# A four-layer transformer kernel on one core: re-ordered joined finish, outputs and first items loaded one stage early, and no start value in the counters of four stages

## The chip, the core and the metric

The kernel is one program on one core of a Trainium2 chip. Its time is the device time of one execution in microseconds (us), smaller is better. The engines are named as in the profile: PE (matmuls), DVE (vector), ACT (activations), POOL (GpSimd) and SP, the engine that in this kernel issues every DMA. They work side by side and wait for each other through semaphores.

## What is computed

Four residual blocks on x of shape 4 x 1024 x 128, cut from the reference:

```
x = x + LN(attn0(LN(x)))      # 16 heads of 8, scores clipped to +-10, causal softmax, output projection
x = x + LN(ffn0(LN(x)))       # RMS norm, latent attention with RoPE, RMS norm, 8 experts top 2 and a shared one
x = x + LN(attn1(LN(x)))      # 16 heads of 8, causal softmax
x = x + LN(ffn1(LN(x)))       # low rank: 128 -> 32 -> 512, gelu, 512 -> 32 -> 128
```

## The kernel before

**Stages.** After a setup (weights loaded, two of them folded together) the program runs nine stages, each a block of five instruction streams, with a barrier over all engines between two stages (`end_phase`, which also gives the semaphores back):

- p0 `project_heads8`: LN of x, q, k and v of attn0, each q and k split into three bf16 parts, stored to device memory (`q8_d`, `k8_d`, `v8_d`)
- a0 `attention`, clipped: 16 items of 4 heads of one sequence; outputs go to `o_d`
- fp `finish_and_project_latent`: joins the end of attn0 (softmax division, output projection, LN, residual add) with the start of ffn0 (RMS norm, latent projections, RoPE products and sums)
- am latent attention, fl its finish, me the experts
- p1 `project_heads8`, a1 `attention` (unclipped: it also finds the row maxima first), ff `finish_and_ffn`

The stages p0, p1, fp and ff go over 8 chunks of 512 tokens; the attentions go over 16 items. `x_res` holds x in SBUF throughout.

**What sets the order.** Nothing schedules: each engine runs its instructions in the order in which the code writes them. In p0 and p1 SP stores every chunk with 7 DMAs (one of v, three of q, three of k). An item of a0 or a1 is loaded with 25 DMAs (`load`, L695 and L698), two items ahead of its use. Before the change the first stretch of an attention's SP stream loads items 0 and 1; in a1 it then also writes eight small rows of minus ones (L737) from a tile that POOL sets (L955).

**The joined finish.** fp and ff are software pipelines. In step c of fp (c from -4 to 7) different chunks are in different phases: outputs of chunk c+4 are turned by PE (L1175) and divided by DVE (`normalise`, L1368 and L1372), chunk c+3 is turned (L391), copied by ACT (`copy_normalised`, L1257) and projected (L1192) into one PSUM bank, chunk c+2 gets its LN: statistics by DVE (L261, L270), `norm1.inverse` by POOL (L284 to L293), `apply_act` by ACT (L309), residual add by POOL (`add`, L1303). Chunk c+1 gets statistics of the new x (L1422, L1429), `inverse_rms` by POOL (L1315 to L1322), `apply_rms` by ACT (L1264) and is turned by PE. Chunk c is projected (four slots, L1226), multiplied with the RoPE tables by DVE (L1378), summed by POOL (`join`, L1330) and stored by SP. The output loads (L1126 in fp, L1875 in ff: 512 KB each) are issued inside the stage.

**Counters.** `sem` takes a semaphore and lets SP add BASE = 1 to it, so that every wait is for a value above 1; a stage's first work on the other engines waits for the last of these adds (`s_begin`). L86 is that add.

Of the kernel before, what the change touches and what calls it, by code (L numbers as in the profile page):

```python
# [17 lines left out]
P = 128  # L18
# [57 lines left out]
def build(nc, ins, consts, out):  # L76
    stack = ExitStack()
    with stack:
# [3 lines left out]
        phase_sems = []  # L82

        def sem(name):
# [66 lines left out]
        area_at = [0]  # L151

        def work(*shape, dt=F32, parts=P):

            n = int(np.prod(shape))
            words = n if dt == F32 else (n + 1) // 2
            a = area[0:parts, area_at[0]:area_at[0] + words]
# [18 lines left out]
        with nc.Block() as block:  # L176
# [8 lines left out]
            def _(pool):  # L185
                nc.gpsimd.memset(zero_f[:, :], 0.0).then_inc(c_zero, 1)
                nc.gpsimd.memset(minus_half[:, :], -0.5).then_inc(c_const, 1)
                pool.wait_ge(c_zero, 1 + BASE)
# [48 lines left out]
        class ChunkNorm:  # L237
# [4 lines left out]
            def __init__(self, name, shifted=False):  # L242
# [5 lines left out]
                self.s_bn = sem(name + "_bn")  # L248
                self.s_mv = sem(name + "_mv")
                self.s_ve = sem(name + "_ve")  # L250
                self.s_rstd = sem(name + "_rstd")
                self.s_out = sem(name + "_out")
                if shifted:
                    self.minus_m = work(self.RING, CT)
                    self.s_minus = sem(name + "_minus")
                    self.s_shift = sem(name + "_shift")
# [7 lines left out]
            def aggregate(self, dve, c):  # L264

                dve.wait_ge(self.s_bn, c + 1 + BASE)
                if c >= self.RING:
                    dve.wait_ge(self.s_ve, c - self.RING + 1 + BASE)
# [8 lines left out]
            def inverse(self, pool, c):  # L277

                r = c % self.RING
                pool.wait_ge(self.s_mv, c + 1 + BASE)  # L280
                if c >= self.RING:
                    pool.wait_ge(self.s_out, c - self.RING + 1 + BASE)
# [4 lines left out]
                pool.wait_ge(self.s_ve, c + 1 + BASE)  # L287
                nc.gpsimd.tensor_tensor(self.rstd[:, r, :], self.ve[:, r, :], minus_half[:, :], ALU.pow)\
                    .then_inc(self.s_rstd, 1)
                if self.shifted:  # L290
                    pool.wait_ge(self.s_minus, c + 1 + BASE)
                    pool.wait_ge(self.s_rstd, c + 1 + BASE)
# [3 lines left out]
            def apply(self, dve, c, src, dst):  # L296
                r = c % self.RING
                dve.wait_ge(self.s_rstd, c + 1 + BASE)
# [5 lines left out]
            def apply_act(self, act, c, src, dst):  # L304

                r = c % self.RING
                act.wait_ge(self.s_shift, c + 1 + BASE)
# [104 lines left out]
        def project_heads8(name, wq, wk, wv):  # L412
            area_at[0] = 0
# [7 lines left out]
            s_pad = sem(name + "_pad")  # L421
            s_T = sem(name + "_T")
            s_xT = sem(name + "_xT")
            s_qk = sem(name + "_qk")
            s_v = sem(name + "_v")
            s_p1 = sem(name + "_p1")
            s_r1 = sem(name + "_r1")
            s_p2 = sem(name + "_p2")
# [1732 lines left out]
```

## Time and profile before

| | |
|---|---|
| median of 3 runs (lowest to highest) | 2126.24 us (2120.15 to 2126.86) |
| the profiled execution: its time, its span | 2121.03 us, 2119.3 us |
| busy: PE, DVE, ACT, POOL | 1711.0, 1302.4, 1140.3, 667.7 us |
| p0 from 40.8, a0: PE from 105.5 to 397 | us from the start of the span |
| fp: PE from 410.8, stage ends at about 555 | |
| p1 from 1482.1, a1: PE from 1546.1 to 2010 | |
| ff: PE from 2023.1 to 2110 | |

The span is from the first to the last instruction. In the rows below a time at the left is counted from the start of the span; "busy" is the time in which an engine executes, and what stands in square brackets is how long the engine had been idle before and who ended it.

### The profile page before, as it was taken

What the parts mean: (1) busy time and instruction counts of PE and PEld (TensorE: products, weight loads), DVE (VectorE), ACT (ScalarE), POOL (GpSimd) and SP (SyncE); (2) the same over time, 40 slices, a digit from 0 to 9 for tenths busy, and PEclk for the clock granted to TensorE, in tenths of its full rate; (3) what the DMA queues carried; (4) which work ended last, traced back from release to release, by engine and by line L of the source; (5) the groups of instructions that cost most, each with busy time, mean ns of one, the idle gap of its engine ahead of it and who ended that gap; (6) DMA issues with size and microseconds to landing.
All of it is one profiled execution on the core that took longest, in us unless ns stands there. A gap on an engine that the chain in (4) does not pass through costs nothing. (4 is left out here: it accounts for less than half of the span.)

```text
span 2119.3 us, 42361 instructions
## 1 busy us (share of the span) xinstructions
PE 1711.0 (81%) x12384; PEld 717.4 (34%) x12384; DVE 1302.4 (61%) x2506; ACT 1140.3 (54%) x1786; POOL 667.7 (32%) x1222
## 2 busy tenths in 40 slices
PE   3487787578269999999999777997569989899757
PEld 3222222243123433433344373553323323233233
DVE  1478878456266665665666044554478878788255
ACT  1599999433015554554555443331617767677736
POOL 2455555268511222222222100010702222222245
PEclk9899999789659999998999888899859999999959
DMA  3632222335511312222230130000521212122031
GB/s 92 222 89 74 74 74 55 83 91 142 115 26 37 71 37 52 56 47 52 47 61 22 61 120 0 0 0 1 200 61 48 56 40 53 46 53 53 17 80 41
DMA packets 91455, 135.14 MB, mean 64 GB/s; under 512 B 26289, under 2 KB 55345, under 8 KB 91186
## 3 DMA queue, kind: packets, MB, share of 16 engines
q1 hardware_dynamic: 91282, 132.86, 24.4%
q8 instruction: 106, 1.74, 0.4%
q14 instruction: 67, 0.55, 0.1%
HBM read 78.30 MB, written 54.39 MB: 63 GB/s over the span
## 5 line engine op out<-in xcount | busy, mean ns | idle before, releaser
L893 ACT ACTIVATE q_buf<-ps 128x1024 f32<-128x1024 f32 (+1 forms) x1152 | 863.7, 822 | 557.9 <-PE ps L780 556.7
L977 DVE TENSOR_REDUCE o_sb<-ps 128x1 f32<-128x512 f32 (+3 forms) x864 | 719.2, 866 | 302.6 <-PE ps L809 196.4
L941 POOL TENSOR_SCALAR_AFFINE_SELECT q_buf<-q_buf 128x256 f32<-128x256 f32 x768 | 364.3, 499 | 850.8 <-ACT q_buf L893 704.5
L829 PE MATMUL ps<-q_buf,v_buf 128*16 128x512 f32 (+7 forms) x4608 | 464.0, 498 | 56.7 <-POOL q_buf L941 54.2
L780 PE MATMUL ps<-q_buf,k_buf 49*128 49x512 f32 (+3 forms) x1536 | 326.2, 526 | 6.5 <-issue 6.5
L780 PE MATMUL ps<-q_buf 48*128 48x512 bf16 (+7 forms) x1536 | 261.2, 333 | 67.6 <-ACT q_buf L893 31.6
L1029 DVE TENSOR_SCALAR q_buf<-q_buf 128x1024 f32<-128x1024 f32 x288 | 215.7, 754 | 69.1 <-ACT q_buf L893 63.8
L780 PEld LDWEIGHTS ps<-q_buf 48*128 48x128 bf16 (+1 forms) x1536 | 76.7, 94 | 318.1 <-ACT q_buf L893 226.2
L780 PEld LDWEIGHTS ps<-q_buf,k_buf 49*128 49x128 f32 x1536 | 133.6, 191 | 136.9 <-ACT q_buf L893 66.6
L829 PEld LDWEIGHTS ps<-q_buf,v_buf 128*16 128x16 f32 (+1 forms) x4608 | 97.2, 100 | 230.7 <-issue 115.9
L802 PE MATMUL ps<-k_buf,q_buf 48*128 48x512 bf16 (+3 forms) x768 | 120.3, 346 | 65.1 <-POOL q_buf L913 31.4
L802 PE MATMUL ps<-q_buf 48*128 48x512 bf16 (+3 forms) x768 | 122.3, 347 | 34.1 <-DMA v_buf<-v_d 24.1
L809 PE MATMUL ps<-causal_bf,ident_bf 128*128 128x128 bf16 x1024 | 120.3, 233 | 1.8 <-issue 1.8
L802 PEld LDWEIGHTS ps<-k_buf,q_buf 48*128 48x128 bf16 x768 | 39.7, 97 | 181.6 <-DVE o_sb L977 128.9
L809 PEld LDWEIGHTS ps<-causal_bf,ident_bf 128*128 128x128 bf16 x1024 | 61.2, 101 | 97.6 <-issue 97.6
L391 PE MATMUL ps<-identity,q_buf 128*128 128x128 f32 x192 | 36.4, 320 | 58.6 <-ACT q_buf L309 34.5
L309 ACT ACTIVATE q_buf<-ps,q_buf 128x128 f32<-128x128 f32 x64 | 24.1, 459 | 72.0 <-POOL q_buf L293 71.9
L802 PEld LDWEIGHTS ps<-q_buf 48*128 48x128 bf16 x768 | 39.8, 96 | 64.4 <-DMA v_buf<-v_d 24.3
L1640 ACT ACTIVATE q_buf<-ps 128x512 f32<-128x512 f32 (+1 forms) x40 | 23.8, 596 | 69.8 <-PE ps L1706 69.6
L1794 DVE TENSOR_TENSOR q_buf<-ps,q_buf 128x512 f32<-128x512 f32 (+1 forms) x40 | 27.6, 690 | 54.7 <-ACT q_buf L1640 54.5
L1378 DVE TENSOR_TENSOR q_buf<-ps,k_buf 128x512 f32<-128x512 f32 (+1 forms) x80 | 49.4, 677 | 15.6 <-PE ps L1226 15.6
L1722 PE MATMUL ps<-w_wd,q_buf 128*128 128x128 f32 (+1 forms) x320 | 59.0, 337 | 0.0
(173 smaller groups left out, 1576.0 us busy)
## 6 DMA issues: line engine op xcount, KB each, us to landing
q_buf<-q_d SPq DMA_DIRECT2D x384, 32.0 KB
q_buf<-k_d SPq DMA_DIRECT2D x384, 32.0 KB
q_buf<-qm_d SPq DMA_DIRECT2D x32, 384.0 KB
qm_d<-pr_buf SPq DMA_DIRECT2D x80, 128.0 KB, 2.4
v_d<-q_buf SPq DMA_DIRECT2D x16, 512.0 KB, 3.1
v_buf<-v_d SPq DMA_DIRECT2D x32, 256.0 KB
o_d<-pr_buf SPq DMA_DIRECT2D x128, 64.0 KB, 2.1
q_buf<-o_d SPq DMA_DIRECT2D x16, 512.0 KB, 6.0
```

The costliest lines, as they stand in the source:

```text
L391: i = nc.tensor.transpose(ps[:, bank, t * P:(t + 1) * P], src[:, t, :], identity[:, :])
L780: mm = nc.tensor.matmul(ps[:, bank + w, off * P:(off + nq) * P], keys(rows, s, p, k), qs[rows, s, p, q0 * P:(q0 + nq) * P], start=True, st ...
L802: mm = nc.tensor.matmul(ps[:, bank[pr], o_ * P:(o_ + nk) * P], (qm if latent else qs)[rows, s, p, q * P:(q + 1) * P], km[rows, s, kk] if l ...
L809: mm = nc.tensor.matmul(ps[:, bank[pr], (o_ + nk - 1) * P:(o_ + nk) * P], ident_bf[:, :], causal_bf[:, :], start=False, stop=True, skip_gr ...
L829: mm = nc.tensor.matmul(ps[VW * j:VW * j + V_ROWS_OUT, o_bank + half % O_BUFS, lo * P:(lo + nq) * P], v, units(i, r, j)[:, 0, off * P:(off ...
L893: nc.scalar.activation(units(i, g, WIDE * e, WIDE), ps[:, bank:bank + WIDE, :], ACT.Exp, scale=scale).then_inc(s_e, 1)
L941: nc.gpsimd.affine_select(out=blk, in_=blk, compare_op=ALU.is_ge, fill=0.0, base=0, pattern=[[0, 2], [1, P]], channel_multiplier=-1)\
L977: nc.vector.tensor_reduce(to, sc, AX_X, ALU.max).then_inc(s_mr, 1)
L1029: nc.vector.tensor_scalar(two, two, float(np.exp(-10.0)), float(np.exp(10.0)), ALU.max, ALU.min).then_inc(s_clip, 1)
L1378: return nc.vector.tensor_tensor(to[0:rows, (ROTS * c + m) % PR, :], ps[0:rows, bank, :], table[tab][:, (c % 2) * CH:(c % 2 + 1) * CH], AL ...
L1722: i = nc.tensor.matmul(ps[:, 6 + u, t * P:(t + 1) * P], hT[0:rows, u, j, t * P:(t + 1) * P], w_sb["wd"][0:rows, j, :], start=(j == 0), sto ...
L1794: nc.vector.tensor_tensor(hT[0:rows, u, j, :], ps[0:rows, 4 + r, :], silu[0:rows, r, :], ALU.mult).then_inc(s_h, 1)
```

## The change

1. **Four stages without a start value.** A new `count` takes a semaphore without the add on SP; p0, p1, fp and ff use it, and every `+ BASE` and `s_begin` wait in them is gone. The attentions, fl and me keep `sem`.
2. **First items one stage early.** p0 and p1 work in another part of `area` (from word 8192), and SP loads item 0 of the coming attention after the stores of chunk 3 and item 1 after those of chunk 5. The attention's SP stream then waits for two long-lived semaphores and adds their value to its own. In p1 SP also writes the eight rows of minus ones after chunk 0; POOL sets their source tile in p1 before it clears `v_pad`.
3. **First outputs one stage early.** At the end of a0 and a1, ahead of the last item's store, SP loads the outputs of chunks 0 to 3 into `o_ahead`; fp and ff load only chunks 4 to 7. The buffer in fp has 4 slots instead of 3.
4. **fp re-ordered.** ACT: `copy_normalised` ahead of `apply_act`. POOL: `inverse_rms` ahead of `norm1.inverse`, and no `add`. DVE: it has the add, and the statistics stand at the end of the step before, those of the new x first.
5. A memset of 2048 words by POOL during the setup.

The core of the diff:

```diff
+        def count(name):
+            phase_sems.append(nc.alloc_semaphore(name=name))
+            return phase_sems[-1]
...
+        def load_item8(sp, seq, i, n, s, done):
+            for pr in range(2):
+                for to, d, term in ((qs8, q8_d, QTERM), (ks8, k8_d, KTERM)):
+                    for t in range(6):
+                        sp.dma_start(to[64 * pr + 8 * t:64 * pr + 8 * t + 8, s, :, :],
+                                     d[bass.ds(seq, 1), term[t], i, pr, :, :, :]
+                                     .rearrange("n d h t -> (n d) h t")).then_inc(done, 16)
+            sp.dma_start(vs8[:, s, :, :], v8_d[bass.ds(n, 1), :, :, :].rearrange("n p k w -> (n p) k w"))\
+                .then_inc(done, 16)
...
# project_heads8, SP, at the end of chunk c
+                        if c == 0 and minus_rows:
+                            sp.wait_ge(ahead_set, 1)
+                            for s in range(NB):
+                                for pr in range(2):
+                                    sp.dma_start(ks8[64 * pr + MD:64 * pr + MD + 3, s, :, :],
+                                                 minus_one.rearrange("p (a t) -> p a t", a=2)).then_inc(ahead_one, 16)
+                        if c in (3, 5):
+                            n = (c - 3) // 2
+                            for r in range(2):
+                                sp.wait_ge(s_st[r], 16 * 7)
+                            load_item8(sp, 0, n, n, n, ahead_item[n])
...
# attention, SP
-                        load(0, 0, 0)
-                        load(0, 0, 1)
+                            for s in range(2):
+                                sp.wait_ge(ahead_item[s], 16 * n_loads * (1 if clip else 2))
+                                sp.sem_inc(s_ld[s], 16 * n_loads)
...
+                    def rest():
+                        if not latent:
+                            for a in range(2):
+                                sp.wait_ge(s_ost[a], 16 * STORES * NQ + BASE)
+                            for c in range(AHEAD):
+                                load_output8(sp, c, ahead_out[c])
+                        store(BATCH - 1, NQ - 1)
...
# finish_and_project_latent, DVE, one step
+                        if there(c + 2):
+                            add(c + 2)
                         if there(c):
                             products_q(c, 1)
+                        if there(c + 2):
+                            collect2(c + 2)
+                        if there(c + 3):
+                            dve.wait_ge(s_y, c + 4)
+                            norm1.collect(c + 3, ps[:, y_bank, :].rearrange("p (t c) -> p t c", c=C))
+                        if there(c + 2):
+                            aggregate2(c + 2)
+                        if there(c + 3):
+                            norm1.aggregate(dve, c + 3)
```

**Place one: SP in p0, stores of chunks 3 and 4.** Before, SP goes from the stores of one chunk to those of the next:

```order
L550 DMA v_d<-q_buf 128x4x256
L556 DMA q_d<-q_buf 128x512 x3
L556 DMA k_d<-q_buf 128x512 x3
L550 DMA v_d<-q_buf 128x4x256
L556 DMA q_d<-q_buf 128x512 x3
```

Now, with the new file's line numbers (L579 and L585 are the stores, L438 and L441 the loads of an item):

```order
L579 DMA v_d<-q_buf 128x4x256
L585 DMA q_d<-q_buf 128x512 x3
L585 DMA k_d<-q_buf 128x512 x3
L438 DMA q_buf<-q_d 8x2048 x6
L438 DMA q_buf<-k_d 8x2048 x6
L438 DMA q_buf<-q_d 8x2048 x6
L438 DMA q_buf<-k_d 8x2048 x6
L441 DMA v_buf<-v_d 128x512
L579 DMA v_d<-q_buf 128x4x256
```

25 DMAs stand between the stores of two chunks; the same follows after chunk 5, and both again in p1.

**Place two: POOL in a full step of fp.** Before: `norm1.inverse`, `inverse_rms`, three joins, the add, two joins:

```order
L284 TENSOR_SCALAR q_buf<-q_buf 128x4
L286 TENSOR_SCALAR q_buf<-q_buf 128x4
L288 TENSOR_TENSOR q_buf<-q_buf,minus_half 128x4
L293 TENSOR_TENSOR q_buf<-q_buf 128x4
L1315 TENSOR_SCALAR q_buf<-mv_xx 128x4
L1316 TENSOR_SCALAR q_buf<-mv_xx 128x4
L1319 TENSOR_TENSOR q_buf<-q_buf,minus_half 128x4
L1322 TENSOR_TENSOR q_buf<-q_buf 128x4
L1330 TENSOR_TENSOR pr_buf<-q_buf 48x512
L1330 TENSOR_TENSOR pr_buf<-q_buf 128x512 x2
L1303 TENSOR_TENSOR x_res<-x_res,q_buf 128x512
L1330 TENSOR_TENSOR pr_buf<-q_buf 128x512 x2
```

Now (L1345 to L1352 are `inverse_rms`, L300 to L309 `norm1.inverse`):

```order
L1345 TENSOR_SCALAR q_buf<-mv_xx 128x4
L1346 TENSOR_SCALAR q_buf<-mv_xx 128x4
L1349 TENSOR_TENSOR q_buf<-q_buf,minus_half 128x4
L1352 TENSOR_TENSOR q_buf<-q_buf 128x4
L300 TENSOR_SCALAR q_buf<-q_buf 128x4
L302 TENSOR_SCALAR q_buf<-q_buf 128x4
L304 TENSOR_TENSOR q_buf<-q_buf,minus_half 128x4
L309 TENSOR_TENSOR q_buf<-q_buf 128x4
L1360 TENSOR_TENSOR pr_buf<-q_buf 48x512
L1360 TENSOR_TENSOR pr_buf<-q_buf 128x512 x4
```

The four small operations of `norm1.inverse`, on which ACT's `apply_act` waits, stand behind those of `inverse_rms`, and the add has left the engine.

**Place three: ACT in the same step.** Before: `apply_act`, `copy_normalised`, `apply_rms`, two copies of latents, the turned copy:

```order
L309 ACTIVATE q_buf<-ps,q_buf 128x128 x4
L1257 ACTIVATE q_buf<-ps 128x512
L1264 ACTIVATE q_buf<-x_res,q_buf 128x128 x4
L1279 ACTIVATE pr_buf<-ps 128x512
L1279 ACTIVATE k_buf<-ps 128x512
L1272 ACTIVATE q_buf<-ps,w_ln 128x512
```

Now:

```order
L1293 ACTIVATE q_buf<-ps 128x512
L325 ACTIVATE q_buf<-ps,q_buf 128x128 x4
L1300 ACTIVATE q_buf<-x_res,q_buf 128x128 x4
L1315 ACTIVATE pr_buf<-ps 128x512
L1315 ACTIVATE k_buf<-ps 128x512
L1308 ACTIVATE q_buf<-ps,w_ln 128x512
```

The copy for chunk c+3 (L1293) now stands ahead of the four norm operations of chunk c+2 (L325).

## Rows read from the trace of the kernel before

**Rows 1.** Busy time of each engine over the span, from the page.

```profile
PE 1711.0 (81%) x12384; PEld 717.4 (34%) x12384; DVE 1302.4 (61%) x2506; ACT 1140.3 (54%) x1786; POOL 667.7 (32%) x1222
```

**Rows 2.** Timeline around the start of a0: start us, us taken, engine, line.

```profile
76.86 1.43 SPq L556 DMA_DIRECT2D k_d<-q_buf  x3
...
88.96 1.44 SPq L556 DMA_DIRECT2D k_d<-q_buf  x3
...
94.54 1.99 SPq L695 DMA_DIRECT2D q_buf<-q_d  x6
...
103.06 2.01 SPq L695 DMA_DIRECT2D q_buf<-q_d  x6
...
105.47 1.46 PE L780 MATMUL ps<-q_buf 48*128 48x512 bf16 x8 [24.43 <-DMA v_buf<-v_d]
```

**Rows 3.** Timeline of SP and PE in p1 and at the start of a1.

```profile
1497.53 0.38 SPq L550 DMA_DIRECT2D v_d<-q_buf  x1
...
1529.42 1.43 SPq L556 DMA_DIRECT2D k_d<-q_buf  x3
...
1546.07 1.03 PE L802 MATMUL ps<-q_buf 48*128 48x512 bf16 x4 [24.14 <-DMA v_buf<-v_d]
...
1552.01 5.60 SPq L737 DMA_DIRECT2D q_buf<-k_buf  x8
```

**Rows 4.** Groups of instructions by line: count, busy us, mean ns, idle before.

```profile
L286 POOL TENSOR_SCALAR q_buf<-q_buf 128x4 f32<-128x4 f32 x48 | 11.9, 247 | 13.2 <-DVE q_buf L270 10.0
...
L2042 DVE TENSOR_TENSOR x_res<-x_res,q_buf 128x512 f32<-128x512 f32 x8 | 5.4, 675 | 3.7 <-ACT q_buf L309 3.7
...
L955 POOL MEMSET k_buf<- 3x2048 bf16 x1 | 1.8, 1794 | 7.9 <-POOLq L93 7.9
```

**Rows 5.** Timeline: first work of p0, fp (POOL, then PE), am (POOL), ff (PE).

```profile
40.84 0.87 DVE L261 BATCH_NORM_STATS2 q_buf<-x_res 128x6 f32<-128x128 f32 x4 [1.95 <-SPq L86]
...
405.17 0.31 POOL L1334 MEMSET q_buf<- 128x256 f32 x1 [9.29 <-SPq L86]
...
410.81 1.09 PE L1175 MATMUL ps<-identity,q_buf 64*128 64x64 f32 x8 [13.74 <-DMA q_buf<-o_d]
...
556.07 3.51 POOL L951 MEMSET k_buf<- 128x4096 f32 x1 [0.97 <-POOLq L93]
...
2023.08 1.09 PE L1892 MATMUL ps<-identity,q_buf 64*128 64x64 f32 x8 [13.13 <-DMA q_buf<-o_d]
```

**Rows 6.** Timeline of fp: one full step, then the starts of two later ones.

```profile
458.01 0.23 POOL L284 TENSOR_SCALAR q_buf<-q_buf 128x4 f32<-128x4 f32 x1 [0.56 <-DVE q_buf L270]
...
460.09 0.23 POOL L1315 TENSOR_SCALAR q_buf<-mv_xx 128x4 f32<-128x4 f32 x1
...
461.48 0.61 ACT L1257 ACTIVATE q_buf<-ps 128x512 f32<-128x512 f32 x1
...
462.10 1.65 ACT L1264 ACTIVATE q_buf<-x_res,q_buf 128x128 f32<-128x128 f32 x4
...
463.80 0.66 PE L391 MATMUL ps<-identity,q_buf 128*128 128x128 f32 x4 [0.50 <-ACT q_buf L1264]
...
466.85 0.36 DVE L1368 RECIPROCAL q_buf<-ps 128x32 f32<-128x32 f32 x1 [4.25 <-PE ps L1175]
...
472.00 0.23 POOL L284 TENSOR_SCALAR q_buf<-q_buf 128x4 f32<-128x4 f32 x1 [0.56 <-DVE q_buf L270]
...
512.57 0.23 POOL L284 TENSOR_SCALAR q_buf<-q_buf 128x4 f32<-128x4 f32 x1 [0.56 <-DVE q_buf L270]
...
525.81 0.23 POOL L1315 TENSOR_SCALAR q_buf<-mv_xx 128x4 f32<-128x4 f32 x1
```

**Rows 7.** Windows of fp: PE, PEld, DVE, ACT, POOL busy; PEclk; DMA share; GB/s.

```profile
411.00:421.00 10.00, 7.19 (x44) 5.98 (x43) 3.10 (x9) 0.60 (x1) 0.00 (x0) 0.50 1.05 240
...
456.00:470.00 14.00, 12.10 (x58) 6.25 (x56) 9.68 (x33) 5.17 (x12) 10.77 (x15) 1.00 0.57 160
...
511.00:524.00 13.00, 9.40 (x20) 2.90 (x19) 7.45 (x26) 4.68 (x11) 9.89 (x14) 0.87 0.65 152
```

**Rows 8.** Timeline of ff: a DVE add and a small POOL operation that meets it.

```profile
2084.70 0.66 DVE L2042 TENSOR_TENSOR x_res<-x_res,q_buf 128x512 f32<-128x512 f32 x1
2084.87 0.57 POOL L286 TENSOR_SCALAR q_buf<-q_buf 128x4 f32<-128x4 f32 x1 [2.80 <-DVE q_buf L270]
```

More of the change, by code:

```diff
@@ L82, in build @@
         phase_sems = []
+        AHEAD = 4
+        ahead_out = [nc.alloc_semaphore(name=f"ahead_out{c}") for c in range(AHEAD)]
+        ahead_item = [nc.alloc_semaphore(name=f"ahead_item{n}") for n in range(2)]
+        ahead_one = nc.alloc_semaphore(name="ahead_one")
+        ahead_set = nc.alloc_semaphore(name="ahead_set")
         def sem(name):
@@ L420, in project_heads8 @@
             v_pad = work(PR, NQ, CT, QUAD, VS)
[L421 to L428, printed above, removed]
-            s_p3 = sem(name + "_p3")
-            s_vp = sem(name + "_vp")
-            s_st = [sem(name + f"_st{r}") for r in range(PR)]
-            s_begin = sem(name + "_begin")
+            s_pad = count(name + "_pad")
+            s_T = count(name + "_T")
+            s_xT = count(name + "_xT")
+            s_qk = count(name + "_qk")
+            s_v = count(name + "_v")
+            s_p1 = count(name + "_p1")
+            s_r1 = count(name + "_r1")
+            s_p2 = count(name + "_p2")
+            s_p3 = count(name + "_p3")
+            s_vp = count(name + "_vp")
+            s_st = [count(name + f"_st{r}") for r in range(PR)]
             with nc.Block() as block:
@@ L762, in store @@
                                          o_two[VW * j:VW * j + VS, i % 2, :]).then_inc(s_ost[i % 2], 16)
-                    run_items(sp, item, first, lambda: store(BATCH - 1, NQ - 1))
+                    def rest():
[5 more added lines that the diff above has]
+                        store(BATCH - 1, NQ - 1)
+                    run_items(sp, item, first, rest)
                     for a in range(2):
@@ L1100, in finish_and_project_latent @@
-            s_rot = sem(name + "_rot")
-            s_lat = sem(name + "_lat")
-            s_st = [sem(f"{name}_st{u}") for u in range(2)]
-            s_xx = sem(name + "_xx")
-            s_begin = sem(name + "_begin")
+            s_tab = count(name + "_tab")
+            s_pad = count(name + "_pad")
+            s_ld = [count(f"{name}_ld{r}") for r in range(AHEAD)]
+            s_turn = count(name + "_turn")
+            s_rd = count(name + "_rd")
+            s_on = count(name + "_on")
+            s_T2 = count(name + "_T2")
@@ L1105, in finish_and_project_latent @@
+            s_vp = count(name + "_vp")
+            s_vst = [count(f"{name}_vst{u}") for u in range(2)]
+            s_mm = count(name + "_mm")
+            s_pr = count(name + "_pr")
+            s_rot = count(name + "_rot")
+            s_lat = count(name + "_lat")
+            s_st = [count(f"{name}_st{u}") for u in range(2)]
+            s_xx = count(name + "_xx")
             STEPS = range(-4, CHUNKS)
@@ L1169, in turn_outputs @@
                     def turn_outputs(c, half):
-                        pe.wait_ge(s_ld[c % LOADS], 16 * (c // LOADS + 1) + BASE)
+                        if c < AHEAD:
+                            pe.wait_ge(ahead_out[c], 16)
+                        else:
+                            pe.wait_ge(s_ld[c % AHEAD], 16)
                         if 2 * c + half > 0:
-                            pe.wait_ge(s_on, 2 * c + half + BASE)
+                            pe.wait_ge(s_on, 2 * c + half)
                         for t in range(HALF):
@@ L1823, in finish_and_ffn @@
             area_at[0] = 0
+            hold[0] = True
             norm1 = ChunkNorm(name + "a", shifted=True)
@@ L1886, in turn_outputs @@
                     def turn_outputs(c, half):
-                        pe.wait_ge(s_ld[c % LOADS], 16 * (c // LOADS + 1) + BASE)
+                        if c < AHEAD:
+                            pe.wait_ge(ahead_out[c], 32)
+                        else:
+                            pe.wait_ge(s_ld[c % AHEAD], 16)
                         if 2 * c + half > 0:
-                            pe.wait_ge(s_on, 2 * c + half + BASE)
+                            pe.wait_ge(s_on, 2 * c + half)
                         for t in range(HALF):
```

461 lines of the change are left out of this document (210 added, 251 removed).

## The prediction

> **What bounds the kernel now.** The page first: PE is busy for 1711 us of the span, and no other engine is near it [rows 1]. That share belongs to the attentions, whose inner loops the change leaves alone. So I read the timelines at the places that the change touches: the stage starts, where the other engines stand still until SP is done with something, and the steps of fp.
>
> At the start of a0 SP issues stores without a pause: from the k stores at 76.86 to those at 88.96 are three chunks, 4.03 us each. Its last issue ends at 90.40, the barrier follows, and the first load is issued at 94.54. Item 0 takes SP from 94.54 to 103.06, 8.52 us of issuing, and PE starts at 105.47, on the last of these loads [rows 2]. So in p0 it is SP's issuing, not the arithmetic, that ends the stage. a1 begins in the same way at 1546.07 [rows 3]. fp and ff start on the first output load, PE at 410.81 and 2023.08 [rows 5].
>
> In fp a full step is one closed chain, with hardly a gap: POOL's norm1.inverse begins at 458.01 and the next one at 472.00, 13.99 us later. Between them: POOL to 460.09, ACT's apply_act, its copy (461.48) and apply_rms (462.10), PE turning x (463.80), the last slot and the outputs, DVE from 466.85 with normalise, the last products and the statistics, which release POOL again [rows 6]. What the change adds to this chain or takes from it is paid in each step.
>
> **The change part by part.** All sums are against the profiled execution's own 2121.03 us (span 2119.3); it lies 0.25% under the median of 2126.24.
>
> *Counters.* p0's first work comes 1.95 us after the setup, held by SP's adds; am's comes 0.97 us after fp's last work, by the barrier alone [rows 5]. The difference, 0.98 us for p0's 22 semaphores, is 0.045 us each. p0 and p1 gain 1.0 each, fp and ff, with 40 and 41 semaphores, 1.8 each.
>
> *Items one stage early, a0.* The 25 issues per item do not vanish, they move into a queue that is already the last to finish. SP ends p0 later by 2 x 8.52 = 17.0, less the 1.0 of the counters: 16.0. Everything behind moves with it: SP reaches a0 at 94.54 + 16.0 = 110.5, finds both items there, and PE starts at about 110.7 instead of 105.47: **+5.2**. Before, only item 0's load stood ahead of PE; item 1's was hidden behind PE's work, and now it stands in front of the barrier. Bounds: the extra issues let the stores drain, which could give back some of the 4.03 us of a chunk (I allow 1.2 in all), or loads beside stores are issued a tenth slower (+1.7): +4 to +7.
>
> *The same in a1.* First store at 1497.53 - 1.0 + 1.8, since POOL's minus-one memset (1.79 us [rows 4]) now stands ahead of the clearing of v_pad and the third norm, for which ACT waits: 1498.3. Then chunk 0's stores 3.9, the eight rows 5.60 [rows 3], seven chunks at 4.03 = 28.2, two items 17.0: 1553.0. From SP's last issue to its first one in the attention are 4.14 us (90.40 to 94.54 [rows 2]), and 0.1 to PE: 1557.3 against 1546.07 [rows 3], **+11.2**. Before, p1's last store was issued by 1530.85 and item 1 and the eight rows went out beside PE. Upward I allow 2; downward 5, if seven chunks in a queue with room cost SP only 3.3 each (its own busy time when it is not pushed back, estimated from 1529.42 + 1.43 less the waits); +6 to +13.
>
> *Outputs one stage early.* The four loads are issued while item 15 is computed, SP has nothing else to do there; if this cover were gone they would cost what they cost now. PE in fp can start at 405.17 - 1.8 + 0.2 = 403.6 instead of 410.81 [rows 5]: **-7.2**. ff has the same wait, 13.13 against 13.74 us, and one semaphore more: **-7.2**. The later loads wait for a free slot as before. Bounds -5.5 to -8.
>
> *fp's order.* Per full step: apply_act now waits for two POOL groups instead of one, +2.08 (458.01 to 460.09); the copy leaves ACT's part of the chain, -0.62 (461.48 to 462.10) [rows 6]; the add joins DVE's part between normalise and the last products, +0.68 by the same add in ff [rows 4]. POOL is not the bound (10.8 of 14 us busy [rows 7]), so that its freed 1.26 us buys nothing. "Shifted one step" changes no distance: the statistics stood at the head of a step and stand at the tail of the one before. Sum +2.1 per step, 16.1 us instead of 14.0. Six steps (-1 to 4) give 12.8. Less 0.9 in step 0, where PE's first slots set the pace, and 0.6 in step 4, where nothing is left to normalise and the add falls into a wait; plus 0.3 for the add in step -2; plus 1.3 in step 5, where PE today idles once and then runs at the lower clock (granted 0.87 in that window; 1.00 in a full step [rows 7]): 512.57 to 525.81, 13.24 us [rows 6]; its new order is 13.3 at full clock, and PE will idle longer. **+13.0**; bounds 0 and +18, the upper if PE falls to 1.2 GHz in two more steps, at 2.5 each.
>
> *Setup memset:* under the 24 us of weight loads, nothing; uncovered 1.8.
>
> Sum: 5.2 + 11.2 - 7.2 - 7.2 + 13.0 = **+15.0**, 2136.0 for the profiled execution, 2141 for the median.
>
> **The rivals.** *A, the loads hide.* If issuing in p0 and p1 fell into idle time of SP, a0 would start at 94.54 and a few tenths, -11.7 with the counters, a1 about -10, and the total were 13.0 - 14.4 - 21.7 = -23: **2103**. For it: before, SP waits for chunks in p1 (33.3 us from first to last store for some 28 us of issuing [rows 3]). Against it: in p0 the pitch of 4.03 us is its own, and 17 us of issues are more than any slack. It decides where an item costs SP less than 4.8 us instead of 8.52, since four items then give the 15 us back. The Trainium skill, DMA: Bandwidth & Descriptors, Rules for kernel authors, says to issue a DMA early, compute, and wait late; taken alone it promises this rival's outcome. Its page speaks of the fixed cost of a transfer; that SP's time to issue is the scarce thing here, the trace shows. Chance 0.07.
>
> *B, fp's order costs nothing.* If ACT did not wait for POOL's norm1.inverse, the step would stay near 14 us and the total were +2: **2128**. Against it: the closed chain of 13.99 us. Chance 0.13.
>
> *C, more than forecast.* PE in fp at 1.2 GHz in several steps, since its longest idle time in a step grows from 0.7 to about 2 us and one of 2.4 us stood before today's slow stretch; or the add meets the joins. On the latter the trace has a case: a POOL operation that takes 0.25 us on average [rows 4] took 0.57 beside a DVE add with two SBUF inputs [rows 8]. In my order the add runs between two joins, and pays nothing; met in each step by a 1.27 us join it would be 7 x 1.27 = 8.9. Total +24 to +30: **2152**. The Trainium skill, SBUF — State Buffer, section on the two separate sides, has the shared port pair as a lock for the whole instruction, against such a DVE operation only where the GpSimd one reads SBUF; by that rule, the trace agrees. Chance 0.12.
>
> *D, something unseen that gains*, such as a higher PE clock in the first steps of fp and ff (granted 0.50 today [rows 7]) after the shorter idle time: -5 to -10 on top, total about +7; chance 0.06, half of it under 0.3%.
>
> **How the numbers follow.** The forecast (slower by 10 to 20 us) has 0.62. 0.3%, 6.4 us, is about what a measurement of this kernel can tell. Slower: forecast 0.62, C 0.12, half of D: 0.77. Same: B and the other half of D, less a little for the tail of B: 0.13. Faster: A and what is left: 0.10. The likeliest case's own range is 2134 to 2148; for 8 in 10 I go down to B's low end, 2123, and up to 2154.
>
> **What would show it.** In the changed trace: SP issues in p0 until about 106, and PE starts a0 near 110.7; SP issues in p1 without a pause from chunk 1 on; PE starts fp some 4 us after a0's last store is issued; two POOL groups stand back to back ahead of ACT's apply_act, and the steps of fp are 16.1 us apart. Wrong I am if an item costs SP much less than 8.5 us in p0, if fp's steps stay at 14, or if the first steps of ff change their pace.

## The result

The changed kernel takes 2138.54 us (median of 7 runs, 2133.60 to 2141.29) against 2126.18 us of the kernel before (7 runs, 2120.15 to 2130.19) on the same chip: ratio 1.0063, 95% interval 1.0044 to 1.0082. It is slower by 0.6%, some 13 us. The forecast was 2141. Its profiled execution took 2138.19 us with a span of 2136.3, 17.0 us more than the profiled one of before.

Below, *stage marks* are used, that is the time at which a stage's first piece of work starts on one named engine: the first work of p0 (DVE), of a0 (PE), of fp (PE), of am (POOL), of p1 (DVE), of a1 (PE) and of ff (PE). The distances between them, in us, each from the start times in the timelines:

| from, to | before | changed | difference |
|---|---|---|---|
| p0, a0 | 64.63 | 72.63 | +8.00 |
| a0, fp | 305.34 | 297.84 | -7.50 |
| fp, am | 145.26 | 161.06 | +15.80 |
| am, p1 | 926.00 | 921.94 | -4.06 |
| p1, a1 | 64.00 | 77.86 | +13.86 |
| a1, ff | 477.01 | 469.46 | -7.55 |
| ff, end | 96.22 | 95.84 | -0.38 |

The rest of the 17.0 us is -1.17 ahead of p0's first work. The line between am and p1 holds 0.84 us of p1's counters; the other 3.2 us lie in stages that the change leaves alone (below, on the clock).

The timeline of the changed kernel around the starts of a0 and a1; the columns are start us, us taken, engine, line, operation, and in brackets the idle time before and what ended it:

```profile
71.74 1.43 SPq L585 DMA_DIRECT2D k_d<-q_buf  x3
73.30 2.38 SPq L438 DMA_DIRECT2D q_buf<-q_d  x6
75.72 2.40 SPq L438 DMA_DIRECT2D q_buf<-k_d  x6
78.16 1.99 SPq L438 DMA_DIRECT2D q_buf<-q_d  x6
80.19 1.99 SPq L438 DMA_DIRECT2D q_buf<-k_d  x6
82.21 0.35 SPq L441 DMA_DIRECT2D v_buf<-v_d  x1
82.61 0.43 SPq L579 DMA_DIRECT2D v_d<-q_buf  x1
...
106.69 1.43 SPq L585 DMA_DIRECT2D k_d<-q_buf  x3
...
112.30 1.46 PE L824 MATMUL ps<-q_buf 48*128 48x512 bf16 x8 [32.58 <-SPq L771]
...
1510.25 0.38 SPq L579 DMA_DIRECT2D v_d<-q_buf  x1
...
1514.18 5.58 SPq L593 DMA_DIRECT2D q_buf<-k_buf  x8
...
1564.90 1.45 SPq L585 DMA_DIRECT2D k_d<-q_buf  x3
...
1571.00 1.04 PE L846 MATMUL ps<-q_buf 48*128 48x512 bf16 x4 [36.34 <-SPq L771]
```

The 25 loads of item 0 stand between two stores and take SP from 73.30 to 82.56: 9.3 us, during which no store of chunk 4 can leave. SP's last issue of p0 ends at 108.12 instead of 90.40, and PE begins 4.18 us behind it. It no longer waits for a load [rows 2] but for SP (L771, the wait at the head of the attention's SP stream). Both items had been issued long before, so what is left of this wait is the barrier. In p1 SP issues from 1519.81 to 1566.35 without a pause.

The starts of fp and ff, and the first work of am, same columns:

```profile
410.14 1.08 PE L1212 MATMUL ps<-identity,q_buf 64*128 64x64 f32 x8 [5.33 <-PEq L103]
...
571.20 3.51 POOL L995 MEMSET k_buf<- 128x4096 f32 x1 [0.97 <-POOLq L103]
...
2040.46 1.11 PE L1927 MATMUL ps<-identity,q_buf 64*128 64x64 f32 x8 [5.44 <-POOL q_buf L2039]
```

PE's idle time ahead of fp is 5.33 us instead of 13.74, ahead of ff 5.44 instead of 13.13 [rows 5], that is 8.4 and 7.7 us less. PE's own time in a0, from its first work to its last, is 0.9 us longer (292.5 instead of 291.6), so that the distance from a0 to fp shrinks by 7.5 only.

One full step of fp in the changed kernel:

```profile
460.87 0.23 POOL L1345 TENSOR_SCALAR q_buf<-mv_xx 128x4 f32<-128x4 f32 x1 [0.56 <-DVE mv_xx L1452]
...
462.79 0.23 POOL L300 TENSOR_SCALAR q_buf<-q_buf 128x4 f32<-128x4 f32 x1
...
464.89 1.50 ACT L325 ACTIVATE q_buf<-ps,q_buf 128x128 f32<-128x128 f32 x4 [5.85 <-POOL q_buf L309]
...
466.27 1.65 ACT L1300 ACTIVATE q_buf<-x_res,q_buf 128x128 f32<-128x128 f32 x4
466.53 1.13 PE L1229 MATMUL ps<-w_wout,q_buf 128*128 128x128 f32 x8 [2.29 <-ACT q_buf L325]
...
471.02 0.36 DVE L1392 RECIPROCAL q_buf<-ps 128x32 f32<-128x32 f32 x1 [5.57 <-PE ps L1212]
...
471.75 0.68 DVE L1440 TENSOR_TENSOR x_res<-x_res,q_buf 128x512 f32<-128x512 f32 x1
...
476.76 0.23 POOL L1345 TENSOR_SCALAR q_buf<-mv_xx 128x4 f32<-128x4 f32 x1 [0.56 <-DVE mv_xx L1452]
```

ACT has been idle for 5.85 us when its apply_act is released by the second POOL group. From POOL's start to apply_rms it is now 5.40 us (460.87 to 466.27) instead of 4.09 [rows 6]; from there to DVE's normalise 4.75 as before; from normalise to the next POOL start 5.74 instead of 5.15, the add. The step is 15.89 us, 1.90 more.

The next two full steps take 17.29 and 17.18 us (476.76, 494.05 and 511.23 are the starts). Windows of the changed kernel; columns as in [rows 7]:

```profile
461.00:477.00 16.00, 12.17 (x59) 6.35 (x60) 10.36 (x34) 5.17 (x12) 9.56 (x14) 1.00 0.64 143
477.00:494.00 17.00, 13.29 (x56) 6.89 (x54) 9.97 (x30) 5.28 (x12) 9.22 (x12) 0.90 0.58 131
...
483.30:486.60 3.30, 3.10 (x10) 1.77 (x9) 0.00 (x0) 2.16 (x5) 1.04 (x1) 0.50 0.56 134
500.40:503.70 3.30, 3.30 (x10) 2.04 (x10) 0.00 (x0) 2.35 (x5) 1.23 (x2) 0.50 0.68 163
```

PE runs at 1.2 GHz (granted 0.50) for one short stretch in each of these steps, and each of the two steps is 1.3 to 1.4 us longer than the one at full clock.

### The profile page after: what moved, and what is told of

Read it like the earlier page. It is cut to its first block and busy times, and to the rows that moved or that the text cites. A ratio compares the mean times of both kernels' runs of the same rounds, so it can differ in the third digit from the quotient of the medians.

```text
span 2136.3 us, 42238 instructions
## 1 busy us (share of the span) xinstructions
PE 1715.9 (80%) x12384; PEld 718.0 (34%) x12384; DVE 1308.1 (61%) x2514; ACT 1140.0 (53%) x1786; POOL 658.2 (31%) x1215
## 5 line engine op out<-in xcount | busy, mean ns | idle before, releaser
L1360 POOL TENSOR_TENSOR pr_buf<-q_buf 128x512 f32<-128x512 f32 (+1 forms) x40 | 50.6, 1288 | 36.8 <-DVE q_buf L1402 36.8
```

The source lines that it names most:

```text
L1360: nc.gpsimd.tensor_tensor(values(c, m)[0:rows, :], t_a[0:rows, r, :], t_b[0:rows, r, :], ALU.subtract if m in (1, 3) else ALU.add).then_in ...
```

## The experiments

All medians are set against runs of the kernel before on the same chip. A difference between the totals of two kernels is read from their ratios, 0.1% being 2.1 us; the intervals are 0.12 to 0.29% to either side, so such a difference is uncertain by some 4 to 7 us. The stage marks are those of the one profiled execution.

| kernel | median us | ratio to before (95%) | p0, a0 | fp, am | p1, a1 |
|---|---|---|---|---|---|
| changed | 2138.54 | 1.0063 (1.0044 to 1.0082) | 72.63 | 161.06 | 77.86 |
| fp's old order | 2123.57 | 1.0002 (0.9990 to 1.0015) | 71.07 | 145.25 | 77.48 |
| POOL groups swapped | 2128.90 | 1.0026 (1.0013 to 1.0038) | 71.21 | 153.77 | 77.76 |
| no items ahead | 2121.58 | 0.9990 (0.9976 to 1.0004) | 64.12 | 160.72 | 63.82 |
| neither | 2107.00 | 0.9918 (0.9898 to 0.9939) | 64.24 | 144.51 | 64.43 |
| add on POOL | 2140.74 | 1.0067 (1.0044 to 1.0090) | 71.03 | 158.12 | 77.46 |
| k loads merged | 2144.25 | 1.0093 (1.0064 to 1.0122) | 73.35 | 161.12 | 80.04 |
| counters alone | 2116.36 | 0.9966 (0.9951 to 0.9982) | 63.87 | 145.09 | 64.30 |
| item 0 by SP | 2096.76 | 0.9869 (0.9844 to 0.9893) | 60.38 | 144.53 | 60.89 |
| item 0 by ACT | 2092.55 | 0.9830 (0.9805 to 0.9854) | 56.33 | 145.07 | 57.01 |
| apply_rms first | 2101.56 | 0.9879 (0.9853 to 0.9906) | 64.89 | 139.07 | 64.19 |
| both repairs | 2078.62 | 0.9797 (0.9775 to 0.9819) | 55.90 | 138.60 | 56.38 |
| and values' copy ahead | 2079.78 | 0.9802 (0.9780 to 0.9824) | 56.85 | 136.65 | 56.52 |

### fp's old order

```diff
 # POOL
-inverse_rms(c + 1); norm1.inverse(pool, c + 2); join 0 to 4
+norm1.inverse(pool, c + 2); inverse_rms(c + 1); join 0 to 2; add(c + 2); join 3, 4
 # ACT
-copy_normalised(c + 3); norm1.apply_act(c + 2)
+norm1.apply_act(c + 2); copy_normalised(c + 3)
 # DVE: no add, statistics at the head of the step
```

> The changed kernel with fp's order put back on all three engines (norm1.inverse ahead of inverse_rms, the add on POOL, apply_act ahead of the copy, the statistics at the head of a step); counters, outputs and items stay early. Theory: fp's steps go back from 15.9 to 17.3 us to 14.0, PE's first work of fp to the last POOL work falls from 160.1 us to about 144.3, and the total by about 15.8: some 2122 to 2125, the kernel before within 0.3%. Rival one (fp lost because its first outputs come from another place and one stage earlier, not by the order): the steps stay near 16 and the total at 2138. Rival two (the order costs only half and the rest is the lower clock that the early start brings): fp falls by 6 to 9 only, about 2131.

Measured: 2123.57, ratio 1.0002; fp to am 145.25 us, as before the change. The timeline of POOL in this kernel:

```profile
470.17 0.23 POOL L300 TENSOR_SCALAR q_buf<-q_buf 128x4 f32<-128x4 f32 x1 [0.56 <-DVE q_buf L286]
...
484.16 0.23 POOL L300 TENSOR_SCALAR q_buf<-q_buf 128x4 f32<-128x4 f32 x1 [0.56 <-DVE q_buf L286]
```

13.99 us again, although counters, outputs and items are still changed. The new order (of ACT, POOL and DVE together) costs fp its 15.8 us; both rivals fall.

### POOL's two groups swapped

```diff
-inverse_rms(c + 1); norm1.inverse(pool, c + 2)
+norm1.inverse(pool, c + 2); inverse_rms(c + 1)
```

> The changed kernel with one swap: POOL runs norm1.inverse ahead of inverse_rms again; the add stays on DVE, the copy ahead of apply_act, the statistics at the tail. Theory (the second POOL group is what apply_act waits for): a full step is 14.0 plus the add's 0.6, that is 14.6 us instead of 15.9, fp as a whole 9 to 12 us shorter, total 2126 to 2130. Rival one (the add on DVE is the cost): a step stays at 15.5 or more. Rival two (the lower clock of PE in the last steps is what lengthens them): the steps of 17.2 fall only to 15.9.

Measured: 2128.90, ratio 1.0026, 7.9 us less than the changed kernel; fp to am 7.3 us shorter. Timeline of POOL:

```profile
475.67 0.23 POOL L300 TENSOR_SCALAR q_buf<-q_buf 128x4 f32<-128x4 f32 x1 [0.83 <-DVE q_buf L286]
...
490.50 0.23 POOL L300 TENSOR_SCALAR q_buf<-q_buf 128x4 f32<-128x4 f32 x1 [0.82 <-DVE q_buf L286]
```

The step is 14.83 us: 1.06 less than 15.89, not 1.3. The missing 0.26 is in the brackets: norm1.inverse waits 0.82 instead of 0.56 us, because DVE aggregates the statistics of the new x first, and those of norm1 come second. In the changed kernel this order of the two aggregates costs nothing, since POOL there begins with inverse_rms, behind the first of them. So the 1.90 us of a changed step are 1.31 between POOL's start and apply_rms and 0.59 for the add; the swap takes back the 1.31 and pays the 0.26. That norm1.inverse stands behind inverse_rms is the largest part, as forecast; fp is 7.3 us shorter instead of the expected 9 to 12, and the total was at the slower end of what was expected.

### No items one stage early

```diff
 # project_heads8, SP
-if c in (3, 5): ... load_item8(sp, 0, n, n, n, ahead_item[n])
-if c == 0 and minus_rows: ... 8 rows of minus ones
 # attention, SP, first
-for s in range(2): sp.wait_ge(ahead_item[s], ...); sp.sem_inc(s_ld[s], 16 * n_loads)
+load(0, 0, 0); load(0, 0, 1)          # and the 8 rows behind them in a1
```

> The changed kernel without items one stage early: SP loads items 0 and 1 and the eight rows of minus ones at the start of the attention, as before the change, and POOL sets the rows' source at the end of p1. Counters, outputs and fp's order stay changed. Theory (SP's issuing is the bound of p0 and p1, so that an issue costs there what it takes): PE starts a0 at about 104.3 instead of 112.3 us, and p1 with the start of a1 takes 13.9 us less; total 22 us less, about 2116. Rival (what slowed p0 was contention of transfers, half of it paid again at the stage start): 8 to 12 us less, about 2128.

Measured: 2121.58, ratio 0.9990, that is 15.5 us less than the changed kernel, not 22. In the profiled execution the stage marks do what the theory says: p0 to a0 64.12, p1 to a1 63.82, together 22.5 us less. 5.4 us come back in a0, which no part of this edit touches: from PE's first work in a0 to its first in fp 303.23 us instead of 297.84. The window of a0 in the kernel with the POOL groups swapped (columns as in [rows 7]):

```profile
111.50:408.50 297.00, 234.33 (x2304) 60.03 (x2304) 232.42 (x320) 269.13 (x288) 166.32 (x256) 0.97 0.28 71
```

The same in this kernel:

```profile
104.50:407.00 302.50, 239.83 (x2304) 60.29 (x2300) 232.58 (x320) 269.14 (x288) 166.42 (x256) 0.96 0.28 73
```

And in the kernel with item 0 by ACT (below):

```profile
96.50:400.00 303.50, 241.07 (x2304) 60.37 (x2300) 232.40 (x320) 269.31 (x288) 165.77 (x256) 0.96 0.29 74
```

The same 2304 matmuls keep PE busy for 5.5 and 6.7 us more, while DVE, ACT and POOL do the same work in the same time: the mark of a lower TensorE clock. More on it below.

### Neither of the two

```diff
-fp's new order        +fp's old order
-items one stage early  +load(0, 0, 0); load(0, 0, 1) at the attention's start
```

> Counters and early outputs alone: fp's old order and no items one stage early, so that both losing parts are undone. Theory (the parts add up): 37 us less than the changed kernel, 2100 to 2104, that is 0.990 of the kernel before: about 7.5 us each from fp's and ff's start and 1 us each from p0's and p1's counters. Rival (the parts overlap: one of the losses hid the other, or the early outputs cost a0 and a1 something at their end): less than 30 us together, over 2108.

Measured: 2107.00, ratio 0.9918, 31 us less than the changed kernel. By the ratios the single edits give 13.0 and 15.5, together 28.5. They add up within the intervals. The expected 37 us were too many; in the profiled execution a0 again runs longer (300.70 us instead of 297.84), and am to p1 took 928.95 us instead of 921.94, stages that neither edit touches.

### Counters alone

```diff
 # on the kernel with neither; attention, SP, ahead of the last item's store
-for c in range(AHEAD): load_output8(sp, c, ahead_out[c])
 # fp and ff, SP, first
+for c in range(AHEAD): load_output8(sp, c, ahead_out[c])
```

> Counters alone: like the kernel with counters and early outputs, but the loads of outputs 0 to 3 stand at the start of fp and ff again. Theory: PE starts fp and ff 5.4 us later each than with early outputs (7.2 less the 1.8 of the counters), total 11 us above that kernel, about 2118, 5 to 8 us below the kernel before. Rival (the counters give nothing, because the first work waits for the barrier or a load anyway): PE starts fp as late as before the change, 13.7 us after its last work, and the total is within 0.1% of before.

Measured: 2116.36, ratio 0.9966, 7.2 us less than before. The timeline at the start of fp:

```profile
401.18 0.31 POOL L1359 MEMSET q_buf<- 128x256 f32 x1 [6.50 <-POOLq L103]
...
406.56 1.11 PE L1203 MATMUL ps<-identity,q_buf 64*128 64x64 f32 x8 [10.68 <-DMA q_buf<-o_d]
```

POOL's first work comes 6.50 us after its last one instead of 9.29, PE waits 10.68 us instead of 13.74 [rows 5]. So the counters give fp 2.8 to 3.1 us, some 0.07 us for each of its 40 semaphores and not 0.045, and the early outputs give the other 5.35 (10.68 to 5.33).

### Item 0 alone, issued by SP behind the last store

```diff
 # project_heads8, SP, behind the loop over the chunks
+load_item8(sp, 0, 0, 0, 0, ahead_item[0])
 # attention, SP, first
-load(0, 0, 0)
+sp.wait_ge(ahead_item[0], ...); sp.sem_inc(s_ld[0], 16 * n_loads)
 load(0, 0, 1)                         # and in a1 the 8 rows behind it
```

> Counters and early outputs with fp's old order, and item 0 alone one stage early, issued by SP behind the last store of p0 and p1; item 1 stays in the attention. Theory (SP's issuing is the bound, 8.5 us per item wherever it stands, so that only what follows the last issue can be hidden): the 8.5 us are paid in p0 instead of a0, but the 2.4 us that PE waited for the last load now lie under the barrier: PE starts a0 about 2.3 us earlier than with loads at the stage's start, some 62 us after DVE's first work of p0 instead of 64.2, the same in a1, total 4 to 5 us less than counters and outputs alone, 2102 to 2103. Rival one (loads right behind stores wait for them in the queue): no gain, 2107. Rival two (SP has room in p0 and p1 and the loads hide): 56 to 58 us, total below 2095.

Measured: 2096.76, ratio 0.9869, 10 us less than "neither". Timeline:

```profile
88.80 2.00 SPq L438 DMA_DIRECT2D q_buf<-q_d  x6
...
96.92 0.35 SPq L441 DMA_DIRECT2D v_buf<-v_d  x1
...
100.17 1.46 PE L820 MATMUL ps<-q_buf 48*128 48x512 bf16 x8 [20.33 <-SPq L762]
```

p0 to a0 is 60.38 instead of 64.24: 3.9 us less where 2.3 were expected. PE begins 2.90 us after SP's last issue; between the last issue of p0 and the first load of the attention there were 4.1 [rows 2]. The 1.2 us between the two fit SP's wait for its last store to land, which now lies under the issuing of the loads (a k store lands some 1.9 us after its issue begins); the rest of the gain is PE's wait for the last load. The two stage starts hold 7.4 us. In the profiled execution a0 (297.80 instead of 300.70) and am to p1 (921.89 instead of 928.95) are shorter too, neither by this edit.

### Item 0 alone, issued by ACT

```diff
 # project_heads8, ACT, behind its last activation
+for r in range(2): act.wait_ge(s_st[r], 16 * 7)
+load_item8(act, 0, 0, 0, 0, ahead_item[0])
```

> Counters and early outputs with fp's old order, and item 0 alone one stage early, its 25 loads issued by ACT after its last activation of p0 and p1, beside SP's last stores; item 1 and then nothing else but the eight rows stay with SP in the attention. The bytes, the number of loads and the neighbourhood of the stores are as in the changed kernel; only the queue that issues differs. Theory (SP's time to issue is what p0 and p1 are bound by): the last store is issued no later than without items, PE starts a0 some 9 to 10 us earlier than with loads at the stage's start (at about 95 instead of 104), a1 the same; total 16 to 20 us less than counters and outputs alone, 2087 to 2092. Rival (the transfers themselves get in each other's way): the stores beside the loads take SP as much longer as before, PE starts a0 at 102 or later, total 2100 or more.

Measured: 2092.55, ratio 0.9830, 18.7 us less than "neither". Timeline of both queues and of PE:

```profile
80.95 2.72 ACTq L438 DMA_DIRECT2D q_buf<-q_d  x6
...
88.27 1.46 SPq L588 DMA_DIRECT2D k_d<-q_buf  x3
...
92.01 0.36 ACTq L441 DMA_DIRECT2D v_buf<-v_d  x1
...
96.07 1.46 PE L820 MATMUL ps<-q_buf 48*128 48x512 bf16 x8 [16.23 <-SPq L762]
```

SP's last store is issued by 89.73, in the kernel with neither by 88.59: 25 loads beside the stores of the last two chunks cost these 1.1 us, and between the stores in SP's own queue they cost 9.3. ACT takes 11.4 us to issue them. p0 to a0 is 56.33 us, p1 to a1 57.01, 7.9 and 7.4 less. The transfers are the same; the queue differs, and the loads now stand beside later stores. SP's issuing is what bounds p0 and p1; what the loads cost the stores beside them is about an eighth of what they cost in SP's queue. The Trainium skill, DMA: Bandwidth & Descriptors, says in its rules for kernel authors that spreading DMAs over SP, ACT and GpSimd gives no bandwidth, since they share the DMA engines, and only saves the issuing engine's time; by that rule, the trace agrees, and that time was the bound here.

### k loads merged

```diff
-for t in range(6): sp.dma_start(ks8[8 rows], k8_d[seq, KTERM[t], i, pr])
+for t, m in ((0, 3), (3, 2), (5, 1)): sp.dma_start(ks8[8 * m rows], k8_d[seq, 0:m, i, pr])
```

> The changed kernel with an item's twelve k loads of eight partitions merged into six (24, 16 and 8 partitions each, the same bytes to the same places): 19 DMAs per item instead of 25. Theory one (SP pays per DMA, 0.34 us each): an item costs 6.5 us instead of 8.5 to 9, a0 and a1 start 4 us earlier each, total 8 us less, about 2130. Theory two (SP pays for the bytes or rows that it describes): an item costs 8.5 us as before, total unchanged, 2138.

Measured: 2144.25, ratio 1.0093 (1.0064 to 1.0122). Timeline of SP (here L437 and L441 are the loads, L582 the store of v):

```profile
76.40 1.98 SPq L437 DMA_DIRECT2D q_buf<-q_d  x6
78.42 1.91 SPq L441 DMA_DIRECT2D q_buf<-k_d  x3
...
80.80 0.43 SPq L582 DMA_DIRECT2D v_d<-q_buf  x1
...
86.06 0.43 SPq L582 DMA_DIRECT2D v_d<-q_buf  x1
```

Three DMAs over 48 partitions take SP 1.91 us, six over the same number 1.98: theory one, a fixed price for each DMA, falls. What the time does follow is open. It isn't the partitions, since the one load of v, with 128 of them, takes 0.35 us, and not the bytes, since it moves 256 KB and each of the small ones 32 KB. The count of 25 in my sum was right only because it came with its measured duration. Besides, the chunk of stores behind the merged loads takes 5.26 us (80.80 to 86.06) instead of the 4.12 of the changed kernel, and 4.8 to 5.3 instead of 4.10 to 4.16 at the three other places; why, no run shows. Whether the merged form is slower than the changed kernel in the total is not settled; the intervals overlap.

### The add back on POOL

```diff
 # DVE
-add(c + 2)
 # POOL, behind the third join
+add(c + 2)
```

> The changed kernel with fp's add back on POOL, after the third join, and nothing else changed: POOL still runs inverse_rms ahead of norm1.inverse. Theory (the add lies on DVE's part of the closed chain): a full step is 0.6 us shorter, 15.3 instead of 15.9, fp 4 to 5 us shorter, total about 2134. Rival one (POOL's add of 1.27 us then stands in the chain instead): a step of 15.9 or more. Rival two (the steps are long enough that the add is hidden on either engine): no change, 15.9.

Measured: 2140.74, ratio 1.0067: no gain in the total. Windows of two full steps in this kernel:

```profile
461.00:477.50 16.50, 13.25 (x56) 6.55 (x54) 9.17 (x26) 5.17 (x12) 10.46 (x13) 0.90 0.58 131
495.00:510.00 15.00, 11.76 (x56) 6.02 (x54) 9.46 (x30) 5.17 (x12) 10.46 (x13) 1.00 0.48 113
```

The step that runs at full clock takes 15.29 us (494.74 to 510.03), as the theory has it; the steps with a stretch at 1.2 GHz take 16.99 (460.76 to 477.75, and again to 494.74). fp is 2.9 us shorter, where 4 to 5 were expected: the steps with a stretch fell by 0.2 to 0.3 us only. That this does not show in the median is within the runs' spread of 10 us.

### apply_rms first

```diff
 # on the kernel with no items ahead; fp alone
 # ACT
-norm1.apply_act(c + 2); apply_rms(c + 1)
+apply_rms(c + 1); norm1.apply_act(c + 2)
 # PE
-out_projection(c + 3); turn_x(c + 1); slot(c, 3); turn_outputs(c + 4, 1)
+turn_x(c + 1); slot(c, 3); turn_outputs(c + 4, 1); out_projection(c + 3)
```

> The changed kernel without items one stage early, and fp's new order carried through: ACT runs apply_rms ahead of apply_act, and PE turns x, computes the last slot and turns the outputs ahead of the output projection. Then only one POOL group, inverse_rms, stands ahead of the chain's next link. Theory (the chain POOL, ACT, PE, DVE is closed, and each link is paid): 2.0 us less than the old order and 0.6 to 0.8 more for the add on DVE: steps of 12.6 to 13.0 us instead of 15.9 (new order) and 14.0 (old order), total about 2098 to 2103. Rival (PE, busy 12.1 us per step, or the output projection now late for the statistics becomes the next bound): steps of 14 or more, total 2108 or more.

Measured: 2101.56, ratio 0.9879; fp to am 139.07 us, 22 less than the changed kernel and 6 less than before. The total is 23.6 us under the kernel with no items ahead, from which it differs in fp's order alone. Timeline:

```profile
467.64 0.23 POOL L1337 TENSOR_SCALAR q_buf<-mv_xx 128x4 f32<-128x4 f32 x1 [0.55 <-DVE mv_xx L1444]
...
469.65 1.65 ACT L1292 ACTIVATE q_buf<-x_res,q_buf 128x128 f32<-128x128 f32 x4 [2.74 <-POOL q_buf L1344]
...
472.37 0.63 PE L407 MATMUL ps<-identity,q_buf 128*128 128x128 f32 x4 [1.35 <-DVE q_buf L1426]
...
481.14 0.23 POOL L1337 TENSOR_SCALAR q_buf<-mv_xx 128x4 f32<-128x4 f32 x1 [0.56 <-DVE mv_xx L1444]
```

The step is 13.50 us, between the theory and the rival. apply_rms starts 2.0 us after POOL, but PE's turn of x does not start when it is done (471.30): it waits for DVE's copy of the values out of the same bank. A wait of 1.07 us has taken the place of the one removed.

### Both repairs, and the copy ahead

```diff
 # item 0 by ACT, and in fp
-old order on all engines
+new order with apply_rms first, and PE's out_projection last
```

> Both repairs together: item 0 alone ahead, issued by ACT, and fp's new order carried through (apply_rms ahead of apply_act, PE's turn of x, last slot and turned outputs ahead of the output projection), with counters and outputs as changed. Theory (the two lie in different stages and add up): PE starts a0 near 96, fp from PE's first work to the next stage near 139 us, total 5 to 6 us below the kernel with item 0 by ACT and the old order, 2086 to 2088. Rival (what fp gains comes back elsewhere, for instance as more low clock in fp, or behind it): 2092 or more.

Measured: 2078.62, ratio 0.9797. fp to am 138.60; 6.5 us less than with item 0 by ACT alone, and the totals differ by about as much (7.0 us by the ratios): the two gains add up. The median is some 8 us under the expected 2086 to 2088. The five runs go from 2077.60 to 2092.47, and the profiled one is the slowest.

```diff
 # DVE
-products_q(c, 0); copy_values(c)
+copy_values(c); products_q(c, 0)
```

> As the kernel with both repairs, and in fp DVE copies the values of chunk c ahead of the four products of the first q slot, not behind them. In the carried-through order PE's turn of x idles 1.35 us for this copy of 0.21 us, since it may overwrite the bank only then. Theory (this copy is the link that took the bound over): a full step falls from 13.5 to 12.5 to 12.7 us, fp by 5 to 7, total 2080 to 2083. Rival one (the copy ahead delays the products, and through them the third slot, by its own 0.2 us and the wait on PE's values): 13.5 or more. Rival two (PE, 12.1 us busy in a step, with its other waits is at its limit): 13.2 to 13.5.

Measured: 2079.78, ratio 0.9802. Timeline:

```profile
469.47 0.23 POOL L1341 TENSOR_SCALAR q_buf<-mv_xx 128x4 f32<-128x4 f32 x1 [0.56 <-DVE mv_xx L1448]
...
473.17 0.66 PE L407 MATMUL ps<-identity,q_buf 128*128 128x128 f32 x4 [0.32 <-ACT q_buf L1296]
474.11 1.99 PE L1259 MATMUL ps<-q_buf,w_wq_rope 128*128 128x512 f32 x4 [0.28 <-DVE q_buf L1398]
...
482.51 0.23 POOL L1341 TENSOR_SCALAR q_buf<-mv_xx 128x4 f32<-128x4 f32 x1 [0.56 <-DVE mv_xx L1448]
```

PE turns x as soon as ACT is done. The step is 13.04 us, not 12.6: now the last slot waits 0.28 us for DVE's products, which the copy pushed back. fp is 1.95 us shorter than with both repairs. In the total the two kernels can't be told apart. Both are 2.0% faster than the kernel before and 2.6% faster than the changed one.

## Why the prediction came out right

The sum was +15.0 us; the profiled execution moved by 17.0, the medians by 12.4. The mechanism of every term held. That the sum came so close is in part luck: in the profiled execution the three losses were 6.2 us larger than forecast in all, and 4.2 us came back elsewhere, most of it in stages that the change leaves alone. Term by term:

- **Start of a0**, forecast +5.2, measured +6.8. The mechanism holds: SP's queue is the last to finish, and the items' issues lengthen it. p0 to a0 was to grow by 6.2 (the 5.2, and the 1.0 of the counters ahead of p0's first work) and grew by 8.0 in this execution, by 6.4 to 6.6 in three others with the same p0.
- **Start of a1**, forecast +11.2, measured +13.0 with the counters: at the upper bound. The first store came 17.1 us after DVE's first work instead of 15.5, as forecast. The seven chunks of stores behind it took 0.9 us more in all than 4.03 us each, item 0 took 9.0 us instead of 8.5, and the gap behind the last issue was 4.65 instead of 4.24.
- **Starts of fp and ff**, forecast -7.2 each, measured -7.5 and -7.55 by the stage marks. For fp this agreement hides an error: PE's idle time fell by 8.4 us, beyond the bound of 8, and 0.9 came back in a0's own work. The outputs gave 5.35 us as forecast (5.4); the counters gave 2.8 to 3.1 in fp and 2.4 in ff (PE idle 10.73 us ahead of ff with counters alone) instead of 1.8. The price of a counter (0.045) was taken from p0 against a barrier of 0.97 us, where the barrier costs p0 only 0.74.
- **fp's order**, forecast +13.0, measured +15.8. The step was to be 16.1 us and is 15.89 at full clock: the second POOL group costs 1.9 us instead of 2.08, the add 0.6 instead of 0.68. What was too small is the clock: I gave 1.3 us for step 5 and put "two more steps" into the upper bound; 1.2 GHz came in four short stretches, at 483.3, 500.4, 517.5 and 534.5. With fp's old order there is one or none of them in fp's steps, and with only the POOL groups swapped one. Rival C was half right: the stretches that it named occur, at 1.3 to 1.4 us and not 2.5 a time. Its reason, PE's longer idle time, fits: the longest one in a full step is 2.3 us in the four kernels that have four stretches, and 0.4 to 1.35 us in the ten, the kernel before among them, that have one or none. No run changes the idle time alone, so that the cause is argued and not shown.
- **Unforeseen**, -3.2 us in the stages from am to me, which hold nothing of the change. TensorE was granted 1.2 GHz there for 160.8 us instead of 168.2.

Rival A falls with item 0 by ACT and with no items ahead: an item costs SP 8.5 to 9.3 us wherever it is issued, far over the 4.8 at which it would have paid. Rival B falls with the swap of the POOL groups: ACT does wait for norm1.inverse. The add met no join, as the order said. Rival D did not show: PE's first steps of fp still ran at 1.2 GHz, until 442.3 us against 440.9 before.

## What to carry to other kernels

Before a transfer is moved ahead into an earlier stage, ask whose queue ends that stage: here SP, and item 0 alone from ACT's idle queue, or behind SP's last store, was a gain where two items between SP's stores were a loss. (No run has both items in ACT's queue, or item 0 alone between the stores.) In a closed chain over four engines an operation that is nobody's bottleneck by its busy share still costs its full time once it stands ahead of the next link; put the operation on which the chain waits first on every engine, and follow it through the last one, or the wait only moves. And undo a bundle part by part: here counters and early outputs gave 17 us, fp's order and the early items took 28 to 31.

## What the runs showed of the hardware

**A stage's time depends on short stretches at 1.2 GHz that come and go with nothing in its code.** In a0 the trace's record of the granted clock shows them at 0.50 for about 3.4 us each. Over the changed kernel and the eleven others with early outputs, none of which touches a0's own work: with none, one or two of them a0 takes 297.3 to 298.4 us (five kernels), with three 300.7 to 301.5 (three), with four 303.2 and 303.3, with five 304.4 and 304.8. What one costs can be read from the start times of a0's 320 DVE instructions, compared one by one with the kernel that has no stretch (POOL groups swapped): they fall behind by 1.2 to 1.6 us around each stretch and elsewhere by at most 0.15 (0.4 in one kernel). Some of it can be made up again: of the changed kernel's 2.5 us from two stretches 0.5 are left at the start of fp. Most kernels with a0's start moved forward had three to five, those with items one stage early none to three, but the kernels with item 0 by SP and with counters alone had one; what decides it stays open. The stretches explain why "no items ahead" gave back 5 of its 22 us in the profiled execution: its four stretches cost 6.3 us, nearly all of which stays. The stages from am to me vary in the same way, from 920.1 to 929.3 us, with 156 to 182 us at 1.2 GHz. A single profile of this kernel can't tell a change of less than some 10 us in the total; the marks of the changed stage can.

**Merging loads into fewer DMAs saved the issuing queue next to nothing** (1.91 us for three over 48 partitions, 1.98 for six). ACT's queue took 11.4 us for what takes SP 8.5, while both were issuing.
